# Row maxima of an attention turned by transposes and placed by GpSimd, and matrix tails computed in pairs

## The chip, the cores and the metric

One core of a Trainium2 chip runs the whole program. The metric is the device time of one execution in microseconds: 436.43 us, the median of 3 runs (436.41 to 436.65), for the kernel before.

## The reference

Two layers over x of shape (2, 1024, 256), with a context of 154 tokens. The first is a cross attention with 16 heads of 16; the second mixes three experts, with a router, and a gate. Cut to what matters:

```python
xq, xkv = ada_ln(x_q, t_vec, Wss_q), ada_ln(x_kv, t_vec, Wss_kv)
q = (xq @ Wq + bq).reshape(B, Lq, 16, 16)
k, v = split(xkv @ Wkv + bkv)
attn = softmax(einsum('bqhd,bkhd->bhqk', q, k) / sqrt(16))
x = x_q + (einsum('bhqk,bkhd->bqhd', attn, v) @ Wp + bp)

nx = layer_norm(x)
weights = softmax((nx @ Wq) @ (ctx @ Wk).T / 16)
combined = concat([nx, weights @ (ctx @ Wv), cond])
router_probs = softmax(combined @ router_W + router_b)
h = silu(combined @ e_w1 + e_b1)              # 3 experts, 768 -> 512
routed = sum((h @ e_w2 + e_b2) * router_probs)
g = sigmoid(silu(combined @ gate_w1 + gate_b1) @ gate_w2 + gate_b2)
return x + g * (routed @ out_w + out_b)
```

## The kernel before

Tokens are worked in 4 chunks of 512 (two per batch element), heads in 4 quartets, so the attention has 16 groups g = (chunk, quartet). Semaphores are placed by hand, and so is the order of the work: `EARLY_ORDER` (line 405) for the attention and the precomputed matrices, `L1_ORDER` (line 424) for the experts. Each letter stands for a step, the n-th occurrence of a letter for its n-th step (`PARTS`), and every engine walks the same string (`walk`, line 488) and issues its own share of each step. An engine takes its instructions in order, so a letter that waits holds back all later letters of that engine.

The letters that matter. P, I and J project the queries and split them into a high and a low part in `xq`. R (`rows`, 1459 and 1089) computes the scores of 128 queries against the 154 keys of a quartet in the pair of PSUM banks, and VectorE reduces them to the row maxima in `nm` (128 queries x 4 heads, padded to 32). Each R waits for the reduction of the R before it, as there is one pair of banks. S (`shift`) turns a group's four blocks of maxima: TensorE multiplies each by `negI`, the negated identity, which gives -max with the queries along the columns in `B_P[1]` (line 1480), and ScalarE copies that into the rows 96 to 127 (`SHIFT`) of the two halves of `xq` (line 836). K (`keys`, 1489) computes the scores again with the keys in the partitions; the ones of the key block times those rows subtract the maximum. ScalarE takes the exponential (`keys`, 842). A (`av`) multiplies by the values with 32-column tiles, then by the tail keys. The keys 0 and 2 of a group wait for the first and the second ScalarE copy.

GpSimd clears `SHIFT` behind the last key step of each group (595), adds biases (`xb`, 585, at letter x), builds key blocks (`place` 639, `second` 649, letters r and y), runs Newton steps (660) and splits the experts' first weights piece by piece (`piece` 675, at letter A of groups 2 to 8). VectorE also has the projections' low parts, the layer norms, and the letters u and w of the output projection. f is one of 27 preparations on TensorE, the last six (w2) of eight matmuls each.

m and t (`mpiece`, 1603, 866 and 1157) multiply the second attention's values by the experts' weights, so that the weights of that attention can be applied to the product: 12 pieces (`MP`, line 314) in the banks `M_BANK` (107), four full ones for each batch element and four tail pieces (None, i) of 64 output rows for the last 26 keys of both. ScalarE takes the high part, VectorE the low part. The expert stage (letters H, D, G and their like) runs from `L1_ORDER`.

Of the kernel before, what the change touches and what calls it, by code (L numbers as in the profile page):

```python
# [43 lines left out]
GH = 4  # L44
# [45 lines left out]
def build(nc, dram, out):  # L90
    ctx = ExitStack()
    with ctx:
# [14 lines left out]
        M_BANK = [B_TOK] * 4 + [(B_H[0], B_H[1], B_G)[n % 3] for n in range(8)]  # L107
# [5 lines left out]
        negI = sb("negI", (P, P), F32R)  # L113
# [86 lines left out]
        nm = sb("nm", (P, 2, TJ, 32), F32R, l0)  # L200
        sb("pad_n", (P, 2, TJ, P - 32), F32, l0)
# [71 lines left out]
        zeroed, neg_r, wq_r = sem("zeroed"), sem("neg_ready"), sem("wq_split")  # L273
# [11 lines left out]
        s1_d, mx_d, nm_d = sem("rowscores_done"), sem("max_done"), sem("shift_added")  # L285
# [28 lines left out]
        MP = [(0, i) for i in range(4)] + [(b, i) for i in range(4) for b in (None, 1)]  # L314
        MTAIL = MP.index((None, 3))

        NM0 = 4

        def m_hi(n):

            return n + 1 + sum(b is None for b, _ in MP[0:n + 1])
# [30 lines left out]
        def y_tile(j):  # L352
# [5 lines left out]
            "q": [("wq", 1)],  # L358
            "c": [("kc", t) for t in range(KC)],
            "f": [("prep", n) for n in range(len(PREP))],  # L360
            "P": [("proj", p, k) for p in range(GR // 2) for k in range(KC)],
            "Q": [("parts", gi) for gi in range(NG)],
# [10 lines left out]
            "A": [("av", g) for g in range(GR)],  # L373
            "y": [("second", n) for n in range(6)],
            "x": [("xt", c, h) for c in range(1, NC) for h in range(2)],
# [14 lines left out]
            "o": [("router", c) for c in range(NC)],  # L390
            "i": [("w2_split", e) for e in range(E)],
            "j": [("gsplit", c, k) for c in range(NC) for k in (HB, HB + 1)],
            "H": [("hidden", c, m) for c in range(NC) for m in HORD],
            "k": [("gw2_split",)],
            "h": [("hsplit", c, m) for c in range(NC) for m in range(HB)],
            "B": [("bias", c, e) for c in range(NC - 1) for e in range(E)] + [("bias", NC - 1, e) for e in (0, 2, 1)],
            "D": [("part", c, m) for c in range(NC) for m in range(HB)],
            "G": [("gate", n) for n in range(TJ * NC)],
# [25 lines left out]
        L1_ORDER = (  # L424
            "iijH"
            "H"
            "kjhLH"
            "hlH"
            "hlBhhH"
            "H"  # L430
            "DH"
            "GNDDLhH"
            "FUNDUH"
            "CUECUEH"
            "GWWDhECH"
# [12 lines left out]
            "GhH"
            "H"
            "hUDUhGDLBDTTGhUplDH"  # L450
            "UH"
            "UhhUlhH"
            "jBDNH"
            "FoDNDH"
            "CUjUUDCUhZZH"
            "H"
            "ZEZhH"
            "DEGWhhhH"
            "BWhCH"
            "UDUhCUH"  # L460
            "H"
            "UDEEGhWDH"
            "H"
            "hTDDTGDWBH"
            "UH"
            "TpTUhDGUH"
            "H"
            "UhjhDBH"
            "DjoUDH"
            "ZDGH"  # L470
            "UZXH"
            "UZhUGhH"
            "ZDH"
            "hhBH"
            "hhUUDDUUDH"
            "BDDH"
            "hXGhH"
            "XDhBDGUaUUahUH"
            "haH"
            "hXH"  # L480
            "aeeDeeDDD"
# [76 lines left out]
        def _(pool):  # L558
# [14 lines left out]
            g_.memset(nm[:].bitcast(F32), 0.0).then_inc(zeroed, 1)  # L573
# [85 lines left out]

            def newton(n):  # L660


                y, v, t = rs[:, 0, 0:TJ], rs[:, 1, 0:TJ], rs[:, 2, 0:TJ]
                pool.wait_ge(rg_r, n)
                for i in range(3):
                    link(g_.tensor_tensor(t, y, y, ALU.mult))
                    link(g_.tensor_tensor(t, t, v, ALU.mult))
                    link(g_.tensor_scalar(t, t, 1.5, None, ALU.subtract))
                    ins = g_.tensor_tensor(y, t, y, ALU.mult)
                    if i < 2:  # L670
                        link(ins)
                ins.then_inc(rs_r, 1)
                pool.wait_ge(rs_r, n)
# [24 lines left out]
            walk(EARLY_STEPS, {"parts": parts, "kr": place, "second": second, "prep": prep, "hi": hi, "xt": xb, "keys": keys, "av": av, "rsqrt": newton, "ln_stats": lambda c: newton(NC + c)})  # L698
# [39 lines left out]
        def _(act):  # L738
# [127 lines left out]
            def mpiece(n):  # L866
# [59 lines left out]
            walk(EARLY_STEPS, {"xt": xt, "parts": parts, "kr": blocks, "second": second, "prep": prep, "hi": hi, "shift": shift, "keys": keys, "av": av, "zt": ztr, **first})  # L926
# [4 lines left out]
        def _(dve):  # L931
# [113 lines left out]
            dve.wait_ge(ld["ident"], 16)  # L1045
            V.tensor_scalar(negI[:], ident[:], -1.0, None, ALU.mult).then_inc(neg_r, 1)
# [42 lines left out]
            def rows(g, q):  # L1089
# [3 lines left out]
                if g >= 2:  # L1093
                    dve.wait_ge(nm_d, g - 1)
                V.tensor_reduce(nm[:, g % 2, q, 0:GH].unsqueeze(2),  # L1095
                                pair[:, :, 0:2 * LK].rearrange("p s (a n) -> p s a n", a=2), AXX, ALU.max).then_inc(mx_d, 1)
# [60 lines left out]
            def mpiece(n):  # L1157
# [6 lines left out]
                if b is None:  # L1164
                    V.tensor_tensor(mt[32:64, 0, o], src[0:32, 0:w], mt[0:32, 0, o], ALU.subtract)
                    ins = V.tensor_tensor(mt[0:32, 1, o], src[32:64, 0:w], mt[32:64, 1, o], ALU.subtract)
# [144 lines left out]
            def scale(j):  # L1311

                dve.wait_ge(th_r, TJ * (NC - 1) + j + 1)
# [18 lines left out]
            walk(EARLY_STEPS, {"parts": parts, "wq": wq_split, "val": val, "stats": chunk_stats, "rsqrt": chunk_rsqrt, "norm": norm, "split": xsplit, "rows": rows, "low": low, "prep": prep,  # L1332
# [5 lines left out]
        def _(pe):  # L1338
# [434 lines left out]
```

## Time and profile before

| | |
|---|---|
| median of 3 runs | 436.43 us |
| profiled execution | 436.14 us |
| its span, first to last instruction | 434.1 us |
| TensorE busy | 419.2 us, 97% |
| VectorE busy | 321.4 us, 74% |
| ScalarE busy | 225.5 us, 52% |
| GpSimd busy | 178.5 us, 41% |
| TensorE's granted clock, share of full | 0.999 |

Times are in microseconds unless marked ns. PE is TensorE's matrix multiplication, PEld its weight load, DVE VectorE, ACT ScalarE, POOL GpSimd, SP the engine that issues DMAs. A busy time is the union of an engine's records; a matmul's record is longer than the step to the next one, as matmuls are pipelined. So the price of a matmul in a sequence is read from start to start. L12 is line 12 of the kernel. Most matmuls are recorded at the helper `passes`, L1348, so they are told apart by what they write and read. "<-" before an engine and line names what ended an idle time. An f32 matmul is recorded as two.

### The profile page before, as it was taken

To read this page: it belongs to the slowest core of one execution; us is meant where nothing else is said; L and a number is where in the kernel's file an instruction comes from. 1 tells how busy PE (TensorE), PEld (TensorE's weight loads), DVE (VectorE), ACT (ScalarE), POOL (GpSimd) and SP (SyncE) were. 2 spreads that over 40 slices of the span, in tenths; PEclk is the share of its full clock that TensorE was granted. 3 is DMA by queue.
4 is the path that set the end of the run, shared out by engine and by line. 5 is a ranking of instruction groups with operands and counts; after the bars stand their busy time and mean duration, and the time that the engine had idled before them with its cause. 6 is when DMAs were issued, how large, how long until landed. Compare 5 with 4: busy or idle time off the path is not lost.

```text
span 434.1 us, 7032 instructions
## 1 busy us (share of the span) xinstructions
PE 419.2 (97%) x2383; PEld 327.5 (75%) x2383; DVE 321.4 (74%) x799; ACT 225.5 (52%) x402; POOL 178.5 (41%) x258
## 2 busy tenths in 40 slices
PE   8988899999999999999999999999999999999995
PEld 5756466775666676655788989898898899888885
DVE  7789889888688776489958786795867637764573
ACT  3767878776885674644324645453236552332120
POOL 4276767647423110001167225533536422545355
PEclk9999999999999999999999999999999999999999
DMA  7912503213102000001100000010000100001001
GB/s 278 401 55 70 174 24 98 63 36 98 37 14 61 15 12 14 0 2 28 52 2 1 2 0 2 0 51 1 2 2 1 50 0 2 0 2 48 2 0 48
DMA packets 8177, 18.92 MB, mean 44 GB/s; under 512 B 1008, under 2 KB 2544, under 8 KB 8016
## 3 DMA queue, kind: packets, MB, share of 16 engines
q1 hardware_dynamic: 7200, 15.55, 10.9%
q0 software_dynamic: 656, 2.29, 1.9%
q10 hardware_dynamic: 288, 0.66, 0.4%
q8 instruction: 19, 0.31, 0.3%
q14 instruction: 14, 0.11, 0.1%
HBM read 13.97 MB, written 2.10 MB: 37 GB/s over the span
## 4 chain that ended last, share of the span: by engine, by line
PE 86%; DVE 5%; ACT 4%; issue 3%; DMA 1%; POOL 0%; SPq 0%; POOLq 0%; DVEq 0%; ACTq 0%
PE bank L1348 53%; PE pair L1348 16%; PE pair L1476 4%; PE bank L1519 3%; PE bank L1516 3%; PE bank L1531 2%; DVE nm L1095 1%; DMA wss_sb<-in_wss 1%; PE bank L1368 1%; ACT xq L834 1%; DVE xq L1105 1%; ACT pt L849 1%; PE bank L1542 1%; PE bank L1634 1%; ACT kc L778 1%
## 5 line engine op out<-in xcount | busy, mean ns | idle before, releaser
L709 POOL TENSOR_TENSOR hs<-hid,hs 128x512 fp32r<-128x512 f32 x48 | 63.2, 1319 | 86.9 <-DVE hs L1266 86.7
L917 ACT ACTIVATE hid<-bank,ab 128x512 f32<-128x512 f32 x56 | 38.4, 688 | 87.3 <-PE bank L1348 63.5
L1348 PE MATMUL bank<-nx,w1h 128*128 128x512 f32 x224 | 71.2, 399 | 0.0
L1348 PE MATMUL pair<-w2h,hs 128*128 128x256 f32 x384 | 70.4, 283 | 0.0
L1095 DVE TENSOR_REDUCE nm<-pair 128x4 fp32r<-128x616 f32 x64 | 51.0, 797 | 17.1 <-PE pair L1476 16.0
L1348 PEld LDWEIGHTS pair<-w2h,hs 128*128 128x128 f32 x384 | 60.6, 189 | 1.8
L1348 PE MATMUL pair<-w2l,hs 128*128 128x256 f32 x192 | 54.1, 282 | 0.0
L849 ACT ACTIVATE pt<-bank 128x512 f32<-128x512 f32 x72 | 41.0, 596 | 12.7 <-PE bank L1348 11.7
L1266 DVE CAST hs<-hid 128x512 fp32r<-128x512 f32 x48 | 23.7, 497 | 30.1 <-PE pair L1348 22.0
L1348 PEld LDWEIGHTS bank<-nx,w1h 128*128 128x128 f32 x224 | 39.7, 189 | 6.9
L1348 PE MATMUL bank<-wh,m_ev 128*128 128x512 f32 x112 | 44.1, 394 | 0.0
L1348 PE MATMUL bank<-nx,w1l 128*128 128x512 f32 x112 | 44.1, 394 | 0.0
L1348 PE MATMUL bank<-xq,keys 128*128 128x512 f32 x96 | 38.1, 448 | 0.8 <-ACT xq L840 0.6
L1476 PE MATMUL pair<-keys,xq 128*128 128x308 f32 x128 | 35.1, 355 | 1.9 <-issue 1.3
L1348 PEld LDWEIGHTS pair<-w2l,hs 128*128 128x128 f32 x192 | 36.1, 188 | 0.0
L1476 PEld LDWEIGHTS pair<-keys,xq 128*128 128x128 f32 x128 | 21.5, 189 | 14.8 <-issue 5.9
L601 POOL MEMSET xq<- 32x1024 f32 x14 | 13.3, 947 | 43.1 <-PE bank L1348 42.8
L1105 DVE SCALAR_TENSOR_TENSOR xq<-bank,small_sb,xq 32x512 fp32r<-32x512 f32 x32 | 23.9, 747 | 1.7 <-ACT xq L834 0.7
L1348 PEld LDWEIGHTS bank<-wh,m_ev 128*128 128x128 f32 x112 | 21.0, 188 | 5.0
L1348 PEld LDWEIGHTS bank<-nx,w1l 128*128 128x128 f32 x112 | 21.0, 188 | 4.9
L1301 DVE SCALAR_TENSOR_TENSOR acc<-pair,pr,acc 128x256 f32<-128x256 f32 x44 | 19.6, 477 | 6.0 <-PE pair L1348 6.0
L834 ACT ACTIVATE xq<-bank,small_sb 32x512 fp32r<-32x512 f32 x32 | 21.8, 680 | 4.0 <-PE bank L1348 3.4
(217 smaller groups left out, 896.3 us busy)
## 6 DMA issues: line engine op xcount, KB each, us to landing
xq<-xq SPq DMA_DIRECT2D x15, 128.0 KB, 2.3
stage<-in_w1n POOLq DMA_DIRECT2D x7, 256.0 KB, 3.2
w1e_sb<-in_w1e SPq DMA_DIRECT2D x1, 1792.0 KB, 8.0
x_sb<-in_x SPq DMA_DIRECT2D x3, 512.0 KB, 8.8
stage<-in_w1a SPq DMA_DIRECT2D x3, 512.0 KB, 10.4
stage<-in_ew2T SPq DMA_DIRECT2D x3, 512.0 KB, 4.0
out_x<-x_sb SPq DMA_DIRECT2D x3, 512.0 KB, 2.7
wss_sb<-in_wss SPq DMA_DIRECT2D x2, 512.0 KB, 6.6
```

What stands on the lines that cost most here:

```text
L601: g_.memset(xq[SHIFT, g % 2].bitcast(F32), 0.0).then_inc(xq_0, 1)
L709: g_.tensor_tensor(hs[:, q % 3, 1, :], hid[:, (M1 * c + HORD.index(m)) % 2, :], hs[:, q % 3, 0, :], ALU.subtract).then_inc(hl_r, 1)
L834: A(xq[HI, g % 2, s_, :], B_P[0][r, :], ACT.Identity, bias=small[r, at:at + 1]).then_inc(qh_r, 1)
L849: A(weight(g, k), B_ST[n % 2][:, :], ACT.Exp, scale=DH ** -0.5).then_inc(ex_d, 1)
L917: A(hid[:, n % 2, :], B_H[n % 2][:, :], ACT.Silu, bias=ab1[:, m, c // CPB:c // CPB + 1]).then_inc(h_r, 1)
L1095: V.tensor_reduce(nm[:, g % 2, q, 0:GH].unsqueeze(2), pair[:, :, 0:2 * LK].rearrange("p s (a n) -> p s a n", a=2), AXX, ALU.max).then_inc( ...
L1105: V.scalar_tensor_tensor(xq[LO, g % 2, s_, :], B_P[0][r, :], small[HI, at:at + 1], xq[HI, g % 2, s_, :], ALU.add, ALU.subtract).then_inc(q ...
L1266: V.tensor_copy(hs[:, q % 3, 0, :], hid[:, (M1 * c + HORD.index(m)) % 2, :]).then_inc(hh_r, 1)
L1301: V.scalar_tensor_tensor(acc[:, j, :], y_tile(j), pr[:, c % 2, j, e:e + 1], acc[:, j, :], ALU.mult, ALU.add).then_inc(y_r, 1)
L1348: ins = mm(dst, a, b_, start=first and i == 0, stop=last and i == len(terms) - 1, skip_group_check=free)
L1476: ins = mm(B_S[s][:, 0:2 * LK], xq[:, g % 2, s, P * q:P * q + P], kr[c // CPB][:, gi, 2 * LK * s:2 * LK * (s + 1)], start=True, stop=True)
L1516: mm(B_U[32 * j:32 * j + 32, :], vmain[:, b, GH * gi + j, :], weight(g, j), start=True, stop=False, skip_group_check=True)
```

## The change

Maxima. The reduction writes the negated maxima (`negate=True`). `negI`, its semaphore and TensorE's `shift` go; `nm` is f32. VectorE turns each group's 128x128 in one transpose by blocks of 32x32 into a new tile `nt`: partition 32a + head then holds the maxima of the queries 32a to 32a + 31 of every block. GpSimd places them by four copies a group, one for each a, from the partitions 32a.. to 96.., both halves of `xq` at once. The keys of a group wait, at step 0 alone, for all four copies.

Tails. The four tail pieces become two: a piece has two 64-column tiles of TensorE in one bank, the first in output rows 0 to 63, the second in 64 to 127 (`tail_parts`). ScalarE and VectorE take the same parts as before, now two pairs behind one piece. `MP` has 10 entries.

Orders. Both order strings are new; `score` and the first late matrix piece wait for the queries' low parts and no longer for the shift; `scale` also waits for the router's weights. The work in the expert stage is the same. The bank of the token work is as it was.

```diff
-        M_BANK = [B_TOK] * 4 + [(B_H[0], B_H[1], B_G)[n % 3] for n in range(8)]
+        M_BANK = [B_TOK] * 4 + [(B_H[0], B_H[1], B_G)[n % 3] for n in range(6)]
...
-        nm = sb("nm", (P, 2, TJ, 32), F32R, l0)
-        sb("pad_n", (P, 2, TJ, P - 32), F32, l0)
+        nm = sb("nm", (P, 2, TJ, 32), F32, l0)
+        nt = sb("nt", (P, 2, TJ, 32), F32, l0)
+        sb("pad_n", (P, 2, TJ, P - 64), F32, l0)
...
-        MP = [(0, i) for i in range(4)] + [(b, i) for i in range(4) for b in (None, 1)]
-        MTAIL = MP.index((None, 3))
+        MP = [(0, i) for i in range(4)] + [(None, 0), (1, 0), (1, 1), (None, 2), (1, 2), (1, 3)]
+        MTAIL = MP.index((None, 2))
...
+        def tail_parts(i):
+
+            return [(64 * (j - i), slice(512 * j, min(512 * j + 512, W1N)), min(512, W1N - 512 * j)) for j in (i, i + 1)]
...
         EARLY_ORDER = (
-            "sqscfPQPbIfJrVfRQfRIbcfrgRJfRQVSnRQfRrKKfrKRKnfKRPbPIfJSA"
-            "KfyybKKRKIfKRxJRA"
-            "RsxySRsfKKRPKygKRfKRIfPJnSA"
-            "KfKRKnfKIRKxRA"
-            "yJRxbSRPfyKbKRuKPKRIKfRzuJSA"
-            "sKRwKKRzuKKRuIJA"
-            "RswSzRKPKRKPKgIRKwRJnzfSA"
-            "KRKwKRKfIKRJfRA"
-            "SRPKKnRuKPKRIKuRzxSJA"
-            "RKuzKRKuKRKwIRJzxSsA"
-            "KmsRtKKPKRKLmtPRIJA"
-            "RfSRwKKRwKRKIzKRfSA"
-            "JRKKuRKPuKRIKPRwSJzfKzRKuKKRwzKRIluA"
-            "JRfSRwzRKmRtA"
-            "RKKmNKKltNFSA"
-            "wKKCCKKfKA"
-            "EwWmuWCECTzmuwtEtmzWEttWmuTmwtmtmTtzTwupmzotw"
+            "ssqfcQQPbPIJfrVIVRQcfbRrfgRfJRQSfnrRfrKRfKRfKRPKKnIPSbfA"
+            "JKKfbKKRxRKyfysRIfRxA"
+            "SyJsRKKfgRPfKKRIPKRnSfA"
+            "KKJRfKyRIKnKRxJRySA"
+            "PbRuKKRPfsKzyRKuIKRxSA"
+            "JbfRuKKRsKzKIRKuRSJA"
+            "wKRKgPKRKPIKRwJzRSfA"
+            "RwzRKKwKRKfnKRnSJIA"
+            "fKPKRuKPRKzIuKRxJA"
+            "RSwRuRzKuKRKsxRsKzKSIJmtA"
+            "KKLmRtPKKRzwIRPKRSfJA"
+            "KKRwKRKwIKRJfRSA"
+            "RPuKKRuzKKRPlKRSfJIA"
+            "wKRKuzKRKwIRKuRSzJfKKRmRtKzKRKmRStlA"
+            "NwKNFA"
+            "wKCKCEKWfKEA"
+            "EWCCumWzTTEuwmtztmtwuWmTTtzmuwptmztwo"
...
-            g_.memset(nm[:].bitcast(F32), 0.0).then_inc(zeroed, 1)
+            g_.memset(nm[:], 0.0).then_inc(zeroed, 1)
...
+            def shift(g):
+
+                pool.wait_ge(nt_r, g + 1)
+                for a in range(TJ):
+                    r = slice(32 * a, 32 * a + 32)
+                    g_.tensor_copy(xq[SHIFT, g % 2].rearrange("p s (q a t) -> p s q a t", q=TJ, a=TJ)[:, :, :, a, :],
+                                   nt[r, g % 2].unsqueeze(1).broadcast_to([32, 2, TJ, 32])).then_inc(sh_r, 1)
+                pool.wait_ge(sh_r, TJ * (g + 1))
...
-            def shift(g):
-
-                act.wait_ge(nm_d, g + 1)
-                for s_ in range(2):
-                    A(xq[SHIFT, g % 2, s_, :], B_P[1][0:32, :], ACT.Copy).then_inc(sh_r, 1)
-
...
-                    A(mt[0:32, 0, o], src[0:32, 0:w], ACT.Copy).then_inc(m_h, 1)
-                    A(mt[32:64, 1, o], src[32:64, 0:w], ACT.Copy).then_inc(m_h, 1)
+                    for r, o, w in tail_parts(i):
+                        A(mt[0:32, 0, o], src[r:r + 32, 0:w], ACT.Copy).then_inc(m_h, 1)
+                        A(mt[32:64, 1, o], src[r + 32:r + 64, 0:w], ACT.Copy).then_inc(m_h, 1)
...
-            dve.wait_ge(ld["ident"], 16)
-            V.tensor_scalar(negI[:], ident[:], -1.0, None, ALU.mult).then_inc(neg_r, 1)
...
-                                pair[:, :, 0:2 * LK].rearrange("p s (a n) -> p s a n", a=2), AXX, ALU.max).then_inc(mx_d, 1)
+                                pair[:, :, 0:2 * LK].rearrange("p s (a n) -> p s a n", a=2), AXX, ALU.max, negate=True).then_inc(mx_d, 1)
+
+            def shift(g):
+
+                dve.wait_ge(mx_d, TJ * (g + 1))
+                if g >= 2:
+                    dve.wait_ge(sh_r, TJ * (g - 1))
+                V.transpose(nt[:, g % 2].rearrange("p q h -> p (q h)"), nm[:, g % 2].rearrange("p q h -> p (q h)")).then_inc(nt_r, 1)
...
-            def shift(g):
-                pe.wait_ge(neg_r, 1)
-                if g:
-                    pe.wait_ge(sh_r, 2 * g)
-                for q in range(TJ):
-                    pe.wait_ge(mx_d, TJ * g + q + 1)
-                    ins = mm(B_P[1][0:32, P * q:P * q + P], nm[:, g % 2, q, :], negI[:], start=True, stop=True)
-                ins.then_inc(nm_d, 1)
-
...
-                if k in (0, 2):
-                    pe.wait_ge(sh_r, 2 * g + 1 + k // 2)
+                if k == 0:
+                    pe.wait_ge(sh_r, TJ * (g + 1))
...
-                rows_ = P if b is not None else 32 * B
-                passes(src[0:rows_, 0:w],
-                       [((vt[:, k].rearrange("p b n -> p (b n)") if b is None else vf[:, k, b, 0:P]),
-                         w1e[:, k, 512 * i:512 * i + w]) for k in range(KC)]).then_inc(m_mm, 1)
+                if b is None:
+                    for k in range(KC):
+                        for r, o, w in tail_parts(i):
+                            ins = mm(src[r:r + 64, 0:w], vt[:, k].rearrange("p b n -> p (b n)"), w1e[:, k, o],
+                                     start=k == 0, stop=k == KC - 1, skip_group_check=True)
+                    ins.then_inc(m_mm, 1)
+                else:
+                    passes(src[:, 0:w], [(vf[:, k, b, 0:P], w1e[:, k, 512 * i:512 * i + w]) for k in range(KC)]).then_inc(m_mm, 1)
```

## Rows read from the trace of the kernel before

**Rows 1.** The page's first part: engine, busy us, share of the span, instructions.

```profile
PE 419.2 (97%) x2383; PEld 327.5 (75%) x2383; DVE 321.4 (74%) x799; ACT 225.5 (52%) x402; POOL 178.5 (41%) x258
```

**Rows 2.** Busy time by stage: stretch, its us, then each engine, clock, DMA.

```profile
24.00:100.00 76.00, 69.73 (x419) 46.78 (x418) 65.79 (x136) 58.47 (x112) 50.14 (x94) 1.00 0.25 73
100.00:184.00 84.00, 83.21 (x433) 55.43 (x430) 61.24 (x115) 56.53 (x103) 19.58 (x32) 1.00 0.12 31
184.00:207.00 23.00, 22.03 (x90) 11.82 (x88) 20.00 (x66) 10.39 (x26) 1.12 (x2) 1.00 0.09 21
207.00:429.00 222.00, 222.00 (x1331) 196.82 (x1332) 155.76 (x422) 87.54 (x136) 95.98 (x108) 1.00 0.03 10
```

**Rows 3.** The chain that ended last, expert stage: start, us, what.

```profile
268.02 2.33 PE bank L1348 x10
270.35 1.42 PE pair L1348 x12
```

**Rows 4.** The line of the turning matmuls: ns min/median/max; what they waited for.

```profile
L1486 PE MATMUL bank<-negI,nm x64: 218/225/622, 33.2 to 174.8; 128*32 128x128 f32 x64
...
  DVE nm L1095: 2.0, 6
```

**Rows 5.** The line of ScalarE's copies of the turned maxima: ns min/median/max.

```profile
L840 ACT ACTIVATE xq<-bank x32: 568/578/587, 33.8 to 177.3; 32x512 fp32r<-32x512 f32 x32
```

**Rows 6.** Order of time, first and last group: start, us, engine, instructions.

```profile
33.16 0.59 PE L1486 MATMUL bank<-negI,nm 128*32 128x128 f32 x4
...
33.74 0.52 PE L1476 MATMUL pair<-keys,xq 128*128 128x308 f32 x2
33.79 0.58 ACT L840 ACTIVATE xq<-bank 32x512 fp32r<-32x512 f32 x1 [1.66 <-PE bank L1486]
...
174.54 0.49 PE L1486 MATMUL bank<-negI,nm 128*32 128x128 f32 x4
174.95 1.06 PE L1516 MATMUL bank<-pt,vmain 128*32 128x512 f32 x8
```

**Rows 7.** Lines and a group of VectorE: ns min/median/max, or count, busy us, mean ns.

```profile
L985 DVE TENSOR_SCALAR lnt<-x_sb,mv,rs x32: 402/408/1481, 11.2 to 317.0; 128x256 f32<-128x256 f32 x32
L985 DVE TENSOR_SCALAR lnt<-x_sb,mv,rs 128x256 f32<-128x256 f32 x32 | 16.2, 549 | 7.5 <-PE bank L1634 3.3 <-POOL rs L669 3.3 <-PE pair L1634 0.7
L1095 DVE TENSOR_REDUCE nm<-pair x64: 786/799/801, 25.9 to 171.9; 128x4 fp32r<-128x616 f32 x64
L1136 DVE COPY anr<-bank x4: 280/284/291, 48.2 to 101.3; 128x128 f32<-128x128 f32 x3, 64x128 f32<-64x128 f32 x1
```

**Rows 8.** Lines of GpSimd: ns min/median/max, first and last start, shapes.

```profile
L607 POOL CAST kc<-kc x8: 433/437/550, 20.1 to 46.3; 32x308 fp32r<-32x308 f32 x8
L625 POOL CAST xq<-xq x2: 605/606/606, 21.1 to 21.8; 32x512 fp32r<-32x512 f32 x2
L696 POOL COPY xkv<-xkv x2: 560/620/680, 16.7 to 17.4; 128x256 f32<-128x256 f32 x2
```

**Rows 9.** The chain that ended last, in attention: start, us, what.

```profile
160.80 0.99 PE bank L1516 x8
161.79 1.06 PE bank L1519 x2
162.85 0.28 PE pair L1476 x2
163.13 1.73 PE bank L1348 x8
```

**Rows 10.** TensorE in order of time, in the stage of the precomputed matrices.

```profile
188.93 1.88 PE L1348 MATMUL bank<-w1e_sb,vf 128*128 128x512 f32 x4
190.65 0.60 PE L1531 MATMUL bank<-ident_sb,u 128*128 128x128 f32 x4
191.09 1.03 PE L1348 MATMUL bank<-wp_sb,zt 128*128 128x256 f32 x4
192.05 1.93 PE L1348 MATMUL bank<-w1e_sb,vt 128*64 128x512 f32 x4
193.91 0.44 PE L1542 MATMUL bank<-ident_sb,z 128*128 128x128 f32 x2
```

More of the change, by code:

```diff
@@ L358, in build @@
             "q": [("wq", 1)],
+            "f": [("prep", n) for n in range(len(PREP))],
             "c": [("kc", t) for t in range(KC)],
-            "f": [("prep", n) for n in range(len(PREP))],
+            "Q": [("parts", gi) for gi in range(NG)],
             "P": [("proj", p, k) for p in range(GR // 2) for k in range(KC)],
-            "Q": [("parts", gi) for gi in range(NG)],
             "b": [("stats", c, h) for c in range(1, NC) for h in range(2)],
@@ L373, in build @@
             "A": [("av", g) for g in range(GR)],
+            "x": [("xt", c, h) for c in range(1, NC) for h in range(2)],
             "y": [("second", n) for n in range(6)],
-            "x": [("xt", c, h) for c in range(1, NC) for h in range(2)],
             "u": [("uz", n) for n in range(TJ * NC)],
@@ L456, in build @@
[L456 to L478, printed above, removed]
+            "iH"
@@ new lines, in build @@
+            "H"
+            "jH"
+            "H"
+            "H"
+            "ijhLhkGhH"
+            "lDGNDlH"
+            "NhDhLDFCBCEGUhUUEH"
+            "UH"
+            "WhhDGCECWlTWBEH"
+            "DhDTUUH"
+            "DTWhpiH"
+            "UTH"
+            "olhNUH"
+            "hH"
+            "BFNDjjDH"
+            "DUhUChZUDUZCH"
+            "ZEEH"
+            "GH"
+            "WZCDhhLWCBH"
+            "hDH"
+            "UUEUUH"
+            "hlDDhEWH"
+            "GH"
@@ new lines, in build @@
+            "TTDhDDBWhH"
+            "GTThpH"
+            "DH"
+            "H"
+            "UhUUUBhH"
+            "jH"
+            "DDNljGDUUUH"
+            "hZhDZUH"
+            "FH"
+            "hGNDoH"
+            "DEhCCGDZZhH"
+            "H"
+            "DhBUhEUUUH"
+            "GH"
+            "WTWBDCTDhCWEEWUDH"
+            "TDTUUhhpH"
+            "UH"
+            "hDH"
+            "DhBDGjH"
+            "H"
+            "hH"
+            "jUoDH"
+            "UUH"
+            "hUGH"
@@ L479, in build @@
+            "hZGH"
+            "ZZDXDhZBhUUDDUUH"
+            "BH"
+            "hBDH"
+            "DhhhGhDH"
+            "XGUaXUDXaUhUH"
             "haH"
-            "hXH"
-            "aeeDeeDDD"
+            "aDDeeDeDe"
         )
@@ L697, in _ @@
             pool.wait_ge(x4_r, B)
-            walk(EARLY_STEPS, {"parts": parts, "kr": place, "second": second, "prep": prep, "hi": hi, "xt": xb, "keys": keys, "av": av, "rsqrt": newton, "ln_stats": lambda c: newton(NC + c)})
+            walk(EARLY_STEPS, {"parts": parts, "kr": place, "second": second, "prep": prep, "hi": hi, "shift": shift, "xt": xb, "keys": keys, "av": av, "rsqrt": newton, "ln_stats": lambda c: newton(NC + c)})
             pool.wait_ge(m_h, m_hi(MTAIL))
@@ L925, in _ @@
             first = {"m_taken": mpiece, "nxf": nxf_, "exp": exp, "wsplit": wsplit, "router": router}
-            walk(EARLY_STEPS, {"xt": xt, "parts": parts, "kr": blocks, "second": second, "prep": prep, "hi": hi, "shift": shift, "keys": keys, "av": av, "zt": ztr, **first})
+            walk(EARLY_STEPS, {"xt": xt, "parts": parts, "kr": blocks, "second": second, "prep": prep, "hi": hi, "keys": keys, "av": av, "zt": ztr, **first})
             walk(L1_STEPS, {"nxf": nxf_, "exp": exp, "wsplit": wsplit, "router": router, "hidden": hidden, "gate": gate})
@@ L1311, in scale @@
             def scale(j):
+                dve.wait_ge(pr_r, NC)
                 dve.wait_ge(th_r, TJ * (NC - 1) + j + 1)
@@ L1331, in _ @@
             out_parts = {"uz": uz, "wp": wproj, "m_taken": mpiece}
-            walk(EARLY_STEPS, {"parts": parts, "wq": wq_split, "val": val, "stats": chunk_stats, "rsqrt": chunk_rsqrt, "norm": norm, "split": xsplit, "rows": rows, "low": low, "prep": prep,
+            walk(EARLY_STEPS, {"parts": parts, "wq": wq_split, "val": val, "stats": chunk_stats, "rsqrt": chunk_rsqrt, "norm": norm, "split": xsplit, "rows": rows, "shift": shift, "low": low, "prep": prep,
                               **out_parts, **front_parts})
@@ L1709, in _ @@
             front_parts = {"nxt": nxt, "score": score, "wtr": wtr}
-            walk(EARLY_STEPS, {"xt": xt, "kc": kc_, "val": val, "proj": proj, "rows": rows, "shift": shift, "keys": keys, "av": av, "prep": prep,
+            walk(EARLY_STEPS, {"xt": xt, "kc": kc_, "val": val, "proj": proj, "rows": rows, "keys": keys, "av": av, "prep": prep,
                               **rows_parts, **front_parts})
```

55 lines of the change are left out of this document (15 added, 40 removed).

## The prediction

> **What bounds the kernel now.** I read the page's first two parts, then the busy time by stage, then the chain of waits, then single stretches in order of time. TensorE is busy 97% of the span [rows 1], at the full granted clock [rows 2]. The stages differ [rows 2]. From 207 to 429 us (experts and gate) TensorE never idles, and its pieces follow each other at fixed prices: a hidden block of ten matmuls 2.33, a part of twelve 1.42 us [rows 3]. 56 of one and 48 of the other are 199 of those 222 us; gates, transposes and scores fill the rest. Only less matmul work shortens this stage, and the change takes none there. From 184 to 207 us (the precomputed matrices) TensorE is busy 22.0 and VectorE 20.0 of 23: two engines near their limit. From 24 to 184 us (attention) TensorE shows 152.9 of 160 us, but that flatters it: a matmul's record of 0.39 us covers a step of 0.23, so short waits hide under records. VectorE has 65.8 of 76 us up to 100 and 61.2 of 84 after; ScalarE 58.5 and 56.5; GpSimd 50.1, then only 19.6 [rows 2]. So attention has no single bound: TensorE's order of work sets the pace, and VectorE is a close second in its first half.
>
> **The maxima's way before.** For each of the 16 groups TensorE turns the four blocks of maxima with 4 small matmuls and ScalarE takes them with 2 copies of 578 ns [rows 4, 5]. These 64 matmuls cost more than their length: in 32-column tiles between 128-column ones, the step from a group's first to whatever follows is 0.58 us in the first of the 16 groups and 0.41 in the last [rows 6]. Followed so through the order of time, the 16 steps are 0.41 to 1.02, 9.8 us together, of which about 2.0 is TensorE waiting for the last maximum [rows 4].
>
> **Edit 1, the turn leaves TensorE and ScalarE.** TensorE loses 16 x 0.5 = 8 us of order time, waits apart. ScalarE loses 32 x 0.578 = 18 us; it is not the bound, so I count nothing. That such tiles cost a change-over shows at the tail pieces, which take 0.15 us more than full pieces of as many matmuls (edit 5). The Trainium skill (TensorEngine Tiling (Array Packing), Key Properties) says that a change of tile mode drains TensorE; by that rule a group that stood right before the weighted values, themselves 32 columns wide, saves one change-over less, and with eight such groups the saving would be 7 rather than 8. The trace agrees that there is such a cost, as just told.
>
> **Edit 2, VectorE's transpose.** 16 transposes of 128x128 f32, SBUF to SBUF, are new; no row shows one. A pass from SBUF over 256 columns is 0.41, so 0.20 is the least; the reduction of 616 columns, 0.80, is the most [rows 7]. The nearest, a 128x128 copy, is 0.284, and I take 0.28: 4.5 us of VectorE time. The Trainium skill (VectorE: DVE Perf Modes, The three transpose paths) gives 311 ns for a bf16 one; by that the sum would be 5.0 us.
>
> **Edit 3, GpSimd's copies.** Per group four copies of 32x256, from partitions 32a to 96..127, with a broadcast source in runs of 32. Nearest rows [rows 8]: a 32-partition cast across partitions of 308 columns 0.437 and of 512 columns 0.606, by which 256 columns are 0.39; a broadcast copy with the same runs and 256 columns 0.62. I take 0.45, 1.8 us per group, and keep 0.39 and 0.62. 64 x 0.45 = 29 us of GpSimd. From 24 to 100 us that makes 50.1 + 8 x 1.8 = 64.5 of 76; it fits, if not loosely.
>
> **Edit 4, the keys wait longer.** Block 0 of a group now needs all four copies, where it needed one ScalarE copy. From the issue of the last row block: about 0.45 for its matmuls, 0.80 reduction [rows 7], 0.28 transpose, 4 x 0.45 copies, and some 0.05 for each of three hand-overs (33.75 to 33.79 [rows 6]): 3.5 us. Before: 0.45 + 0.80 + 0.2 + 0.58 + 0.15 = 2.2 us. What covers this is what TensorE has between the last row block and the keys in the written order. Pricing each letter by its steps (A 2.05, R 0.28, a w2 prep 1.73 [rows 9], u 0.44, w 0.96 [rows 10], the rest in the same way), the new order leaves 2.7, 4.6, 2.7, 3.5, 3.4, 4.0, 2.8, 3.9, 3.7, 2.1, 4.6, 3.7, 3.4, 4.6, 2.0, 3.3 us in groups 0 to 15. Against 3.5 the shortages sum to 6 us (groups 9 and 14 are 1.4 and 1.5 short); the old order against 2.2 is short by 1.5. Net +4.5; with copies of 0.39 us +3, with 0.62 +12. Behind the waiting keys stand the next row blocks, and for those VectorE and ScalarE. On GpSimd the copies stand behind the memset of each group, the splits of the expert weights and the bias adds; the new order puts the splits (letter A) mostly behind S, so I add nothing, though y, y and x come just before the third S.
>
> **Edit 5, tails in pairs.** A full piece steps 1.72 us (188.93 to 190.65); a tail piece of 64 output rows, with as many matmuls, 1.87 three times (192.05 to 193.91) and 1.01 once, for the 256-column one: 6.6 us for the four [rows 10]. Now two pieces of eight matmuls in two 64-column tiles. Eight matmuls of 512 columns in four 32-column tiles take 1.06 us together [rows 6], less than four full ones, so separate column tiles do run together; two pairs are then 2 x 1.87 = 3.7, and TensorE saves 2.9 us. ScalarE and VectorE keep all their tail instructions, and VectorE is nearly as full as TensorE here, 20.0 of 23 us [rows 2]. What VectorE does here falls only because one set of router weights (some 2 us of small passes) and its exponential now come before the last attention block. So the stage gains about 2.2, not 2.9.
>
> **The small ones.** The negated identity was one small pass of VectorE in the start, where TensorE waits for loads anyway: 0. The memset keeps its size. The new wait of scale for the router's weights is met long before. The score's and matrices' waits move from the shift to the low parts, earlier: 0. The order of the expert stage is new with the same work, and TensorE idles nowhere in it: 0, plus or minus 1.
>
> **Sum.** -8.0 (edit 1) +4.5 (edit 4) -2.2 (edit 5) +0.7 for VectorE's extra 4.5 us in the part of attention where it has 87% = -5.0. The profiled execution is 436.14 us with a span of 434.1, 0.3 under the median of 436.43; I take the sum from the median: 431.4 us.
>
> **Rivals.** (a) All of TensorE's saving comes home, because the waits for keys fall where others were: -8.0 - 2.9 = -10.9, 425.5 us. For it: TensorE's near 97%. Against it: the shortages above. (b) GpSimd's copies become the path: at 0.62 us each edit 4 costs 12, and -8.0 + 12 - 2.2 = +1.8, 438.2 us, slower. It decides from about 0.56 us a copy, where cost meets saving. For it: the row with the same access pattern [rows 8]. Against it: that row was taken while VectorE worked from SBUF, and the plain casts are far shorter. (c) VectorE becomes the bound of the first half: 65.8 busy + 8 x 0.28 + 0.7 = 68.7; if its idle share of 13% stays, 24 to 100 grows by 3.3 instead of shrinking, and with -1.8 to 184 us and -2.2 behind, it is -0.7: 435.7, no change. The 0.7 is this: VectorE's passes over SBUF alone take 0.41 us as a rule, but up to 1.48 [rows 7], which for the 32 of one kind is 32 x (0.549 - 0.408) = 4.5 us more, beside a GpSimd that is busy 178.5 us in the span; 29 more make 0.7. The Trainium skill (GPSIMD Engine Reference, SBUF interfaces) says that GpSimd contends with VectorE's two-port and two-input SBUF instructions. By that rule both engines lose whenever they meet, and the trace agrees in so far as the long ones stand beside GpSimd work. (d) The 64-column tiles don't run together and the pair is two pieces in series: the tails give nothing, 433.6 us.
>
> **How the numbers follow.** Chances: forecast 0.50 (its own range 429 to 434), (a) 0.15, (b) 0.20, (c) 0.10, (d) 0.05. The range takes in (a) and (b): 425.5 to 438.5. A measurement can tell about 0.2%, 0.9 us, from no change. Faster: 0.50 + 0.15 + 0.05 + half of (c) = 0.75. Same: the other half of (c) and a fifth of (b), 0.09. Slower: 0.16.
>
> **What would show it.** Transposes near 0.28 us, 64 GpSimd copies near 0.45 with a group's four in 1.8; TensorE's waits for xq released by GpSimd, in all some 5 us, longest in groups 9 and 14; two tail pieces of 1.9 us; the first hidden block some 5 us earlier, at about 202.5 us; 222 us from there to the end of the parts, as before. Copies over 0.56 us, GpSimd without gaps before 100 us, or VectorE at 92% there would make it wrong.

## The result and the profile after

The changed kernel takes 439.15 us (median of 4 runs, 438.93 to 440.47) against 436.42 for the kernel before beside it: a ratio of 1.0069, 95% interval 1.0057 to 1.0081. It is 2.7 us slower, where 5.0 us faster was forecast, and lies 0.65 us above the range. The profiled execution took 438.93 us with a span of 437.1. Of all executions below only one is left out of the ratios: it is of one_turn, and took 517.86 us at a granted clock of 0.753.

The page's first part, engine by engine, against [rows 1]:

```profile
PE 415.6 (95%) x2319; PEld 322.8 (74%) x2319; DVE 321.6 (74%) x814; ACT 209.1 (48%) x370; POOL 206.0 (47%) x322
```

TensorE has 64 records less, ScalarE 16 us less busy time, GpSimd 28 us more. The work went where the change sends it; VectorE shows no more in all, though 4.8 us more between 100 and 184 us. The stages, to hold against [rows 2]:

```profile
24.00:100.00 76.00, 66.07 (x355) 41.93 (x354) 64.45 (x137) 46.05 (x89) 58.94 (x111) 0.98 0.23 68
100.00:184.00 84.00, 80.19 (x399) 51.56 (x399) 66.08 (x123) 47.87 (x87) 36.51 (x78) 1.00 0.14 35
184.00:207.00 23.00, 22.78 (x112) 13.96 (x111) 18.71 (x67) 12.67 (x30) 0.96 (x2) 1.00 0.00 1
207.00:429.00 222.00, 221.02 (x1314) 194.89 (x1313) 151.48 (x428) 88.30 (x138) 95.02 (x107) 1.00 0.04 12
```

The columns behind the span are the busy times of TensorE, its weight loads, VectorE, ScalarE and GpSimd. TensorE is busy 6.7 us less between 24 and 184 us than before (146.3 against 152.9), and yet attention ends later: the first hidden block of the experts starts at 210.5 us in TensorE's order of time, against 207.9. From there to the end of the parts it is 221.9 us against 221.4, so nearly all of the loss lies ahead of the experts. TensorE's longest waits:

```profile
PE bank L1364 <- POOL xq L670: 6.0, 8, 1.6
PE pair L1492 <- DVE nm L1102: 4.0, 7, 1.1
```

6.0 us of waiting for the placement and 4.0 for the row reductions. Before, the like waits were 0.6 for ScalarE's copies and, for the reductions, 0.5 ahead of row blocks and 0.6 ahead of turns. The weight loads, which run beside the matmuls, show 11.9 us of waits for the placement; these are in part the same time, so the two don't add up. The prices of the new operations, from their lines (ns min/median/max):

```profile
L670 POOL CAST xq<-nt x64: 392/398/742, 34.9 to 180.5; 32x256 fp32r<-32x256 f32 x64
L1110 DVE STREAM_TRANSPOSE nt<-nm x16: 299/311/313, 34.4 to 178.6; 128x128 f32<-128x128 f32 x16
```

A transpose is 0.31 us and a copy 0.40; four of them in a row take 1.77 us. One place stands out, group 2. In order of time, first GpSimd, then VectorE's turn, then TensorE (start, busy time, engine, line and what it does, with the wait before it in brackets):

```profile
46.70 4.42 POOL L597 TENSOR_TENSOR x_sb<-x_sb,bp_sb 128x256 f32<-128x256 f32 x6
51.18 0.95 POOL L606 MEMSET xq<- 32x1024 f32 x1
52.23 3.80 POOL L635 TENSOR_SCALAR keys<-kc,small_sb 128x616 fp32r<-128x616 f32 x2
56.11 1.41 POOL L597 TENSOR_TENSOR x_sb<-x_sb,bp_sb 128x256 f32<-128x256 f32 x2
57.59 2.20 POOL L670 CAST xq<-nt 32x256 fp32r<-32x256 f32 x4
...
55.77 0.31 DVE L1110 STREAM_TRANSPOSE nt<-nm 128x128 f32<-128x128 f32 x1
...
57.70 0.55 PE L1492 MATMUL pair<-keys,xq 128*128 128x308 f32 x2
59.84 0.73 PE L1364 MATMUL bank<-xq,keys 128*128 128x512 f32 x2 [1.58 <-POOL xq L670]
```

GpSimd works from 46.70 without a break. The maxima were turned by 56.08, and the copies start 1.5 us later behind bias adds. TensorE stands 1.58 us, after which its granted clock drops (stretches of 2 us; the clock is the last column but two):

```profile
58.00:60.00 2.00, 0.42 (x3) 0.17 (x2) 1.82 (x3) 0.94 (x2) 1.62 (x3) 1.00 0.00 0
60.00:62.00 2.00, 2.00 (x21) 1.44 (x22) 0.72 (x6) 1.09 (x2) 0.00 (x0) 0.78 0.00 0
62.00:64.00 2.00, 2.00 (x6) 1.50 (x6) 0.94 (x3) 0.10 (x1) 1.27 (x7) 0.50 0.46 130
64.00:66.00 2.00, 2.00 (x10) 1.62 (x9) 0.80 (x1) 0.99 (x3) 1.22 (x6) 0.87 0.00 1
```

At 0.50 TensorE runs at 1.2 GHz of its 2.4. Just before, it had been busy 0.42 of the 2 us from 58 on. The drop does not always follow: the profiled execution of new_old_experts (below) has the same early order and the same wait of 1.58 us, and stays at full clock:

```profile
62.00:64.00 2.00, 2.00 (x11) 1.41 (x10) 1.39 (x6) 1.03 (x2) 1.07 (x6) 1.00 0.42 115
```

Its span is 436.4 us against 437.1, and it took 438.42. By these two executions the drop in the clock is worth at most some 0.7 of the 2.7 us.

### The profile page after: what moved, and what is told of

It is laid out like the page before. It is cut to its first block, busy times and chain, and to the rows that moved or that the text cites. A ratio compares the mean times of both kernels' runs of the same rounds, so it can differ in the third digit from the quotient of the medians.

```text
span 437.1 us, 6957 instructions
## 1 busy us (share of the span) xinstructions
PE 415.6 (95%) x2319; PEld 322.8 (74%) x2319; DVE 321.6 (74%) x814; ACT 209.1 (48%) x370; POOL 206.0 (47%) x322
## 4 chain that ended last, share of the span: by engine, by line
PE 77%; DVE 7%; POOL 6%; issue 4%; ACT 3%; DMA 1%; POOLq 0%; SPq 0%; DVEq 0%; ACTq 0%
PE bank L1364 48%; PE pair L1364 15%; PE pair L1492 3%; POOL xq L670 3%; DVE nm L1102 3%; PE bank L1526 2%; PE bank L1523 2%; PE bank L1384 1%; DMA wss_sb<-in_wss 1%; DVE xq L1119 1%; POOL x_sb L597 1%; PE bank L1538 1%; ACT pt L857 1%; ACT xq L848 1%; PE bank L1629 1%
## 5 line engine op out<-in xcount | busy, mean ns | idle before, releaser
L1102 DVE TENSOR_REDUCE nm<-pair 128x4 f32<-128x616 f32 x64 | 51.1, 798 | 16.1 <-PE pair L1492 15.0
L1281 DVE CAST hs<-hid 128x512 fp32r<-128x512 f32 x48 | 25.6, 539 | 31.5 <-PE pair L1364 18.2
L670 POOL CAST xq<-nt 32x256 fp32r<-32x256 f32 x64 | 25.9, 404 | 25.2 <-DVE nt L1110 22.2
L1364 PEld LDWEIGHTS bank<-xq,keys 128*128 128x128 f32 x96 | 16.9, 191 | 15.1 <-POOL xq L670 11.9
```

What stands on the lines that cost most here:

```text
L670: g_.tensor_copy(xq[SHIFT, g % 2].rearrange("p s (q a t) -> p s q a t", q=TJ, a=TJ)[:, :, :, a, :], nt[r, g % 2].unsqueeze(1).broadcast_to ...
L1102: V.tensor_reduce(nm[:, g % 2, q, 0:GH].unsqueeze(2), pair[:, :, 0:2 * LK].rearrange("p s (a n) -> p s a n", a=2), AXX, ALU.max, negate=Tr ...
L1281: V.tensor_copy(hs[:, q % 3, 0, :], hid[:, (M1 * c + HORD.index(m)) % 2, :]).then_inc(hh_r, 1)
L1364: ins = mm(dst, a, b_, start=first and i == 0, stop=last and i == len(terms) - 1, skip_group_check=free)
```

## The experiments

### Each edit alone

The tails in pairs alone: the tail edits of the diff in the kernel before, and its early order less four letters (an m and a t for each of the two pieces less).

```diff
-            "EwWmuWCECTzmuwtEtmzWEttWmuTmwtmtmTtzTwupmzotw"
+            "EwWmuWCECTzmuwtEtzWEtWmuTmwtmtTzTwupmzotw"
```

> The kernel before with the tails in pairs alone, its orders kept but for the four letters of the two pieces that are gone (an m and a t each). If the two 64-column tiles run together, TensorE has 2.9 us less in the stage of the precomputed matrices; with VectorE close behind there I expect 1 to 2.5 us less in all, 434 to 435.4. If they run in series: 436.4, within 0.3.

Measured: 435.59 us against 436.39, ratio 0.9984 (0.9976 to 0.9993). That is 0.8 us gained, the most of any kernel here that leaves nothing out. From its trace, TensorE after 184 us:

```profile
195.82 1.93 PE L1628 MATMUL bank<-w1e_sb,vt 128*64 128x512 f32 x8
197.68 1.13 PE L1354 MATMUL bank<-wp_sb,zt 128*128 128x256 f32 x4
...
201.78 0.44 PE L1548 MATMUL bank<-ident_sb,z 128*128 128x128 f32 x2 [1.03 <-DVE x_sb L1126]
```

Eight matmuls step 1.86 us (195.82 to 197.68), just what four took in [rows 10]: the two tiles do run together. But of the 2.9 us freed 2.3 come back as waits for VectorE, as at 201.78; from 184 us on the kernel before has no such wait over 0.2 us. So VectorE gates this stage. Would it help to move VectorE's work out, as the changed kernel does? Against tails_alone:

```diff
-            "wKKCCKKfKA"
-            "EwWmuWCECTzmuwtEtzWEtWmuTmwtmtTzTwupmzotw"
+            "wKKCCKEKWfKA"
+            "wmuWCECTzmuwtEtzWEtWmuTmwtmtTzTwupmzotw"
```

> The tails in pairs alone, as in tails_alone (435.59), and one exponential and one set of router weights (an E and a W) moved before the last attention block, as the changed kernel has them. If VectorE's row of work is what hides the pairs' saving behind 184 us, that gives 1 to 2 us more: 433.5 to 434.6. If something else bounds the stage: 435.2 to 435.9, or more if the exponential holds up the last key blocks.

Measured: 435.90 us, ratio 0.9989 (0.9981 to 0.9998), within the noise of the pairs alone. Moving this one E and W does not give the rest. What would was not found.

The maxima alone, in the old orders; and both edits in the old orders:

> The maxima's way of the changed kernel (VectorE transposes, GpSimd places) in the old orders, tails as before. Theory P: the longer way from the last maximum to the keys costs more than TensorE's 8 us, in any order: 439 to 443. Theory O: the new early order is at fault, above all the 10 us of GpSimd work ahead of the third placement, and the way itself pays: 431 to 434.

> Both edits in the old orders of both stages (less the letters of the two pieces). Theory P: 437 to 441, the new order had repaired part of the loss. Theory O: 430 to 433, well under the changed kernel's 439.15.

Measured: 477.24 us, ratio 1.0930 (1.0908 to 1.0952), and 477.46 us, 1.0912. Neither theory came near. The new way in the old orders costs 41 us, so the new early order is no fault but most of the cure: it takes 38 of them away. Group 3 of maxima_alone shows how such a loss arises; VectorE, then GpSimd, then TensorE:

```profile
69.30 0.80 DVE L1101 TENSOR_REDUCE nm<-pair 128x4 f32<-128x616 f32 x1 [0.53 <-PE pair L1490]
70.02 0.16 DVE L1153 TENSOR_TENSOR ab<-bank,small_sb 128x8 f32<-128x8 f32 x1
70.88 1.52 DVE L1118 SCALAR_TENSOR_TENSOR xq<-bank,small_sb,xq 32x512 fp32r<-32x512 f32 x2 [0.71 <-ACT xq L848]
72.44 0.73 DVE L993 TENSOR_SCALAR lnt<-x_sb,mv,rs 128x256 f32<-128x256 f32 x2
73.09 0.30 DVE L1109 STREAM_TRANSPOSE nt<-nm 128x128 f32<-128x128 f32 x1
...
73.53 1.76 POOL L670 CAST xq<-nt 32x256 fp32r<-32x256 f32 x4 [1.29 <-DVE nt L1109]
...
75.34 0.80 PE L1362 MATMUL bank<-xq,keys 128*128 128x512 f32 x1 [3.22 <-POOL xq L670]
```

The last maximum was there at 70.10, and the turn starts at 73.09. In the old order S stands behind J and n, whose VectorE shares (a wait for ScalarE, 1.52 and 0.73 us) now stand ahead of the turn; as TensorE's step, S did not mind them. And the clock falls behind such a wait:

```profile
72.00:74.00 2.00, 0.12 (x1) 0.00 (x0) 1.36 (x4) 0.60 (x1) 0.65 (x3) 1.00 0.29 66
74.00:76.00 2.00, 0.66 (x2) 0.56 (x3) 0.00 (x0) 0.00 (x0) 1.77 (x4) 0.50 0.00 0
76.00:80.00 4.00, 4.00 (x17) 3.90 (x15) 0.64 (x1) 0.92 (x2) 2.10 (x2) 0.50 0.20 42
```

So I moved nothing but S:

```diff
-            "RsxySRsfKKRPKygKRfKRIfPJnSA"
+            "RSsxyRsfKKRPKygKRfKRSIfPJnA"
```

(likewise in every group where S stood further back)

> The kernel of the maxima alone in the old orders (477.24), with one move: each S right behind its group's fourth R, so that VectorE turns before its low parts and norms, and not after. There the transpose stood 1.77 us after its maximum in the mean, against 0.31 in the changed kernel. Theory that the place of S in VectorE's queue is what the old order lost: 25 us or more less, 440 to 452. Rival, the order of everything else is the loss: 465 or more.

Measured: 453.26 us, ratio 1.0390 (1.0372 to 1.0408). 24 of the 41 us were the place of one letter. The clock multiplies such waits. The mean granted clock of the profiled execution is 0.962 in maxima_alone and 0.984 here, so by an estimate from these and the spans (0.038 x 475.1 and 0.016 x 451.4) 18 and 7 us of full clock are missing; up to 11 of the 24 us are the clock's. For the other 17 us the trace has TensorE wait 8.5 us for the placement; the rest was not followed.

The new early order with the old way of the maxima and the tails in pairs is the counterpart:

> The old way of the maxima (TensorE turns, ScalarE places) and the tails in pairs, in the new early order, where S stands right behind the fourth R. TensorE then waits for each last reduction, 0.8 us and more, before the turn: 16 times 0.8 against the old order's 2.0 us in all. If the new order fits the new way alone: 444 or more. If it is a better order in itself: 436 or less.

Measured: 454.34 us, 1.0423 (1.0377 to 1.0468). TensorE's longest waits there:

```profile
PE bank L1492 <- DVE nm L1100: 13.4, 12, 2.1
```

13.4 us before the turn, as expected (16 times 0.8). Each order fits one way of doing the maxima.

The changed kernel with the old order of the experts alone:

> The changed kernel with the old order of the expert stage. If that order is neutral, as forecast: 439.15 within 0.5. If the new one is a part of the loss: the 0.4 us by which the stage is longer in the trace, or more, 437.5 to 438.7.

Measured: 438.71 us, 1.0060 (1.0044 to 1.0077), against 1.0069 (1.0057 to 1.0081) for the changed kernel. The expert order is neutral within what these runs tell.

### How much of it is the way's length

```diff
-                for a in range(TJ):
+                for a in range(1):
...
-                    pe.wait_ge(sh_r, TJ * (g + 1))
+                    pe.wait_ge(sh_r, g + 1)
```

> The changed kernel with GpSimd placing only the first of a group's four 32-query runs: three quarters of the maxima are not subtracted. Each way from the last maximum to the keys is 3 x 0.46 = 1.4 us shorter and GpSimd has 19 us less. Theory: the length of the way is what TensorE waits for in 12 of 16 groups (6.0 us by the engine, 11.9 by its weight loads); then 5 to 9 us less than 439.15, 430 to 434. Rival: VectorE or the reductions are the bound and the way only takes their place; then less than 2 us, over 437.

Measured: 435.02 us, ratio 0.9978 (0.9965 to 0.9990), so 4.1 us less than the changed kernel, just short of the expected 5. The waits for GpSimd are gone from TensorE's longest, and those for the reductions grew:

```profile
PE pair L1492 <- DVE nm L1102: 5.7, 8, 1.4
```

Taking 16 x 1.4 = 22 us out of the ways, and some 19 us out of GpSimd with them, gives 4.1; the run does not part the two. It also shows how little a faster placement could bring in this order: even with three copies of four left out, this kernel is no better than the pairs alone within the intervals.

Two ways to shorten it in truth. ScalarE takes two of the four copies:

```diff
-                for a in range(TJ):
+                for a in (0, 1):
...
+                act.wait_ge(nt_r, g + 1)
+                for a in (2, 3):
+                    A(xq[SHIFT, g % 2]..., nt[r, g % 2]..., ACT.Copy).then_inc(sa_r, 1)
```

> The changed kernel with the placement shared, two runs by GpSimd and two by ScalarE at once. The way is 0.9 us shorter where ScalarE is free. Theory of the way's length: 3 to 6 us less, 433 to 436. Rival: ScalarE stands before the transpose in its queue and holds up exponentials and query copies, 437 to 442.

Measured: 445.41 us, 1.0222 (1.0203 to 1.0241): the rival. The trace says why:

```profile
103.50 0.38 ACT L882 ACTIVATE zt<-bank 128x256 f32<-128x256 f32 x1
105.87 0.85 ACT L857 ACTIVATE xq<-nt 32x256 fp32r<-32x256 f32 x2 [1.99 <-DVE nt L1121]
```

The placing took 0.9 us, as wished, but ScalarE stands before it for the turn, here 1.99 us and 15.6 us in 12 places of the trace, and everything behind it in its queue stands too. That this is what costs the 6 us was not tested apart.

The letters y, GpSimd's key blocks, moved behind the placement of group 2:

```diff
-            "JKKfbKKRxRKyfysRIfRxA"
-            "SyJsRKKfgRPfKKRIPKRnSfA"
+            "JKKfbKKRxRKfsRIfRxA"
+            "SyyJsRKKfgRPfKKRIPKRnSyfA"
```

> The changed kernel with the key blocks of the second batch (letters y) moved from before the third placement to behind it: GpSimd's queue no longer delays that placement by 1.5 us (nor by the port, 2.2 instead of 1.77), TensorE does not stand 1.6 us there and keeps its full clock from 60 to 65 us, where it fell to half. Theory that this place is a large part: 2.5 to 4 us less, 435 to 436.7. Rival, the loss is spread over all groups: 0 to 1.5 us less, over 437.6.

Measured: 440.46 us, 1.0091 (1.0071 to 1.0110), no gain. The rival was nearer, though even it had expected no loss. In its trace group 2 is mended: the copies start at 56.28, TensorE has no wait there, and the stretch of low clock is gone. But groups 3 and 5 then wait 1.3 and 0.4 us, where the changed kernel shows no wait, so that TensorE waits 6.2 us for the placement in all against 6.0. The span is 437.1 us, as without the move. Six executions spread from 438.91 to 441.39 us, the long ones with a granted clock of 0.994, so the low clock has not gone from all of them.

### What TensorE's time was worth

The forecast's largest term was 8 us of TensorE's order. First, three of four turns left out in the kernel before (ScalarE's copies keep their size; the turn that is left now waits for the last of the four maxima):

```diff
-                for q in range(TJ):
-                    pe.wait_ge(mx_d, TJ * g + q + 1)
+                pe.wait_ge(mx_d, TJ * (g + 1))
+                for q in range(1):
```

> The kernel before with one of the four turning matmuls of a group: the first block's maxima are subtracted from all four blocks. ScalarE's copies read that block four times over and stay 32x512. TensorE loses 48 matmuls, 5 to 6 us by its steps, and nothing else changes. Theory that TensorE's order sets attention's pace, on which the forecast's 8 us rests: 4 to 6 us less than 436.4, 430.5 to 432.5. Rival, that VectorE and the hand-overs set it and TensorE's work there is worth less than its length: 0 to 2.5 us less, 434 to 436.4.

> One_turn once more, for an undisturbed trace: 436.6, no faster than the kernel before, as 10 of 11 executions showed. In the trace the first hidden block starts at 207.5 to 208.5 us as before. If the three earlier turns of a group were hidden in waits: the row blocks and the keys start at the old times in most groups and TensorE's waits are longer by the 5 us. If a new wait ate the saving: one place where it falls behind by several us.

Measured: 436.63 and 436.68 us, ratios 1.0008 (0.9999 to 1.0017) and 1.0007 (0.9998 to 1.0017). Nothing gained. The trace gives the reason. Group 1, the last reduction and what TensorE does, first in the kernel before, then in one_turn_again:

```profile
43.08 0.80 DVE L1095 TENSOR_REDUCE nm<-pair 128x4 fp32r<-128x616 f32 x1
43.66 0.52 PE L1486 MATMUL bank<-negI,nm 128*32 128x128 f32 x4
44.11 0.64 PE L1516 MATMUL bank<-pt,vmain 128*32 128x512 f32 x4
...
43.42 0.80 DVE L1096 TENSOR_REDUCE nm<-pair 128x4 fp32r<-128x616 f32 x1
44.37 0.22 PE L1487 MATMUL bank<-negI,nm 128*32 128x128 f32 x1
44.52 1.07 PE L1517 MATMUL bank<-pt,vmain 128*32 128x512 f32 x8
```

The last maximum is there at 43.88 and at 44.22. Before, TensorE turns the first blocks while VectorE still reduces the last, and goes on to the next work 0.23 us behind the last maximum. The single turn starts 0.15 us behind it, and the next work 0.30. So the three turns left out had stood largely where TensorE waited anyway. Told over the trace, the first turn starts ahead of the end of the last reduction in 14 of the 16 groups, by 0.04 to 0.65 us, 4.4 us together of the 9.8 that the prediction counted. In one_turn_again the single turn starts 0.14 to 0.15 us behind that end in the same 14. Group 15 has no such wait, and there the step from the first turn to the next work falls from 0.41 us [rows 6] to 0.23, about 0.06 for each turn. The probe was weaker than meant. Doubling the turns (each issued twice) tests the other side:

> The kernel before with each of the 64 turning matmuls issued twice: TensorE gains 64 small matmuls of 0.06 to 0.1 us, 4 to 6 us of work; results are the same. If TensorE's work at this place fills waits that are there anyway: 436.4 to 438. If it counts in full one way and not the other: 440 to 443.

Measured: 436.90 us, 1.0011 (1.0002 to 1.0021). 64 matmuls more cost 0.5 us; in group 15 the step is 0.65 us for eight, again 0.06 each.

That left the last turn of a group and the change to 32 columns, so all turns went. ScalarE's copies read what stood in the bank, and no maxima are subtracted:

```diff
-                act.wait_ge(nm_d, g + 1)
+                act.wait_ge(mx_d, TJ * (g + 1))
...
-            def shift(g):
-                pe.wait_ge(neg_r, 1)
...
-                ins.then_inc(nm_d, 1)
```

> The kernel before with no turning matmul at all: ScalarE's copies are as in one_turn, but what they read is left from the start, so no maxima are subtracted; they start on the last reduction itself. In the traces of before and of one_turn_again four turns or one both cost the steps between 0.4 and 0.5 us to the work behind, as the change to 32-column tiles is the cost and not the matmuls. If that fixed cost was in the way: 16 x 0.2 to 0.45, 3 to 7 us less, 429.5 to 433.5, and the forecast's 8 us were roughly there to be had. If TensorE's time at this place is worth nothing: 435 to 436.4.

Measured: 436.59 us, ratio 1.0005 (0.9996 to 1.0014). With no turn at all, a shorter way, and nothing put in its place, the kernel before does not get faster. The stages of its trace, against [rows 2]:

```profile
24.00:100.00 76.00, 67.27 (x383) 44.18 (x385) 65.47 (x136) 57.91 (x111) 49.82 (x93) 1.00 0.25 72
100.00:184.00 84.00, 80.58 (x401) 52.29 (x395) 61.93 (x115) 56.92 (x104) 20.17 (x33) 1.00 0.12 31
```

TensorE is busy 5.1 us less (147.9 against 152.9) in the same 160 us, VectorE the same 127 us: the time taken from TensorE turned into waiting. The last reduction of group 1 ends at 44.35 us and that of group 11 at 137.86, against 43.88 and 137.19 before: ten groups take 93.5 us without a turn and 93.3 with it. The trace is of the slowest execution of this kernel (437.67 us against the median of 436.59), and part of its excess stands right behind that point:

```profile
139.45 0.52 PE L1475 MATMUL pair<-keys,xq 128*128 128x308 f32 x2 [1.30 <-DMA xq<-xq]
```

That DMA was issued at 135.25, 4.2 us earlier, where the median of its line is 2.3 us. The ratio, which goes by the medians, does not rest on it.

The opposite probe takes VectorE's time and leaves TensorE's:

```diff
-                                pair[:, :, 0:2 * LK].rearrange("p s (a n) -> p s a n", a=2), AXX
+                                pair[:, :, 0:2 * LK].rearrange("p s (a n) -> p s a n", a=2)[:, :, :, 0:LK // 2], AXX
```

> The kernel before with each row reduction over 77 of the 154 keys: the maximum is that of half the keys. VectorE loses 64 x about 0.3 us, 20 us, and each row block after another comes that much sooner; TensorE's work is as before. If TensorE's order sets the pace: 0 to 2 us less, over 434.4. If the chain of row block and reduction, or VectorE's load, sets it as much: 4 us or more less, under 432.4.

Measured: 433.10 us, ratio 0.9926 (0.9913 to 0.9940), 3.3 us less, between the two expectations. Its trace has VectorE at 58.2 of 76 us and 51.1 of 84, so some 18 us of VectorE and of the chains through it bought 3.3, where 5 us of TensorE bought none. The run does not part VectorE's load from the length of the chain.

## Why the prediction was wrong

**Edit 1, the step that failed.** The forecast followed TensorE's 16 steps through the order of time, 9.8 us, took off 2.0 for waiting, and put the other 8 on the path. Two things were wrong with it. Of the 9.8 us 4.4, and not 2.0, lie ahead of the end of the last reduction, which the last turn had to wait for anyway. And what is left is worth nothing either: with all turns gone no_turn has a ratio of 1.0005 (0.9996 to 1.0014), so it is between 0.2 us faster and 0.6 us slower than the kernel before. The premise, "TensorE's order of work sets the pace", came from 97% busy, of which the text itself said that it flatters. In attention TensorE has time between row block, reduction, projection, DMA and copy, and the turn lay in it. Rival (a), which rested on the same reading, was the same error. This is measured in the old order. In the new one the turns would have cost TensorE its 13.4 us of waits (old_way_new_order), so what edit 1 is worth there is not measured by itself.

**Edit 3 and 2, the prices.** Right: a copy 0.40 for 0.45 and four in 1.77 for 1.8; a transpose 0.31 for 0.28. The slow copies of rival (b) did not come; that the time came out near its 438.2 us is chance.

**Edit 4, the longer way.** Its mechanism was right. Its size, 6.0 us of waits where 6 were worked out as shortages (5.6 by the list itself), agrees in part by luck: the waits stand in groups 0 to 2, 4, 8, 10, 12 and 14, the longest in group 2, and of the two that were to be longest 14 has 0.94 us and 9 has none. Not priced was what follows behind the waiting keys: TensorE's waits for row reductions grew from 0.5 to 4.0 us. One_copy puts 4.1 us on three quarters of the placement. The text saw y, y and x before the placement of group 2 and gave them nothing; the y made its 1.58 us. As y_late gained nothing, that was not what decided.

**The order as a cover.** To count what stands in TensorE's order between the last row block and the keys was sound. What it left out is that S also has a place in VectorE's queue. The new order had that right; in the old one it cost 24 us.

**Edit 5.** The tiles run together, and TensorE's step is 1.86 us for 1.87. Of the 2.2 us only 0.8 came in the old order, as VectorE gates that stage; the text had seen VectorE at 20.0 of 23 us and still gave it 2.2 on the strength of one moved E and W, which alone brings nothing. The changed kernel was not run without the pairs, so their worth in the new order is not measured.

**The sum as it now stands.** 0 (edit 1) + 3.5 (edit 4, the queues and the clock) - 0.8 (edit 5) = 2.7. The 3.5 is what is left over, not measured by itself, and the sum takes for granted that terms measured in the old order hold in the new one; one_copy's 4.1 for three quarters of the placement fits it. Rival (c), VectorE as the bound, was nearest in kind: VectorE's time is worth something, TensorE's none; but VectorE has 64.5 of 76 us in the first half, no more than before, and so is no bound by itself. What the runs point to is a loop of dependences through TensorE, VectorE and ScalarE as what paces attention. Which of its links is the longest in each group stays open. That expectations missed by 30 us and more for the old orders shows how far hand-written queues, and the clock behind them, can amplify a step's move.

## What to carry to other kernels

Before counting an engine's saved time, take its work out in the old kernel and time that: no_turn, one small edit, would have shown that TensorE's 8 us were worth nothing before anything was built in their place. Take all of it out: one_turn left the one turn that waits, and could not have told. An engine at 97% by its records can be idle wherever dependences run in a loop; ask which wait ends last in that stage. When a step moves to another engine in an order shared by all, look at what stands ahead of it in the new engine's queue, and hold the whole way from the last input to the first consumer against the old one.

## What the runs showed of the hardware

- A turning matmul of 128 columns in a 32-column tile adds about 0.06 us to TensorE's step where nothing else is waited for: 0.23, 0.41 and 0.65 us for one, four and eight in group 15. Doubling all 64 cost 0.5 us. What the change of tile size costs by itself is not isolated.
- Two 64-column tiles in one bank run together: eight 512-column matmuls step 1.86 us, as four do.
- Four independent GpSimd copies of 32x256 across partitions take 1.77 us, 0.46 each in a row. In group 2 they took 2.20, the longest single one 0.74, beside two passes of VectorE from SBUF to SBUF (xh<-xf and xl<-xf,xh); beside its passes that read PSUM, as in group 3 at 68.02 us, they took 1.77.
- A wait of 1.58 us, in a stretch where TensorE was busy 0.42 of 2 us, was followed in one execution by some 4 us at a lower granted clock, down to half, and in another by none. In maxima_alone a wait of 3.22 us (busy 0.12 of 2 us) was followed by at least 4 us at half.
